# Eight batches of a conditioned transformer block on one core: maxima turned by quarters and halves, score blocks in a third bank

## What is computed

```
c6 = silu(c) @ Wc + bc                       # shifts, scales, gates
xm = ln(x) * (1 + sc_msa) + sh_msa
q, k, v = xm @ Wq + bq, xm @ Wk + bk, xm @ Wv + bv
w = softmax((q / DH) @ k.T)                  # per head, 512 x 512
x = x + g_msa * ((w @ v) @ Wo + bo)
xm2 = ln(x) * (1 + sc_mlp) + sh_mlp
x = x + g_mlp * (gelu(xm2 @ W1 + b1) @ W2 + b2)
```

## Time and profile before

| | |
|---|---|
| median of 3 runs | 773.78 us (772.47 to 776.5) |
| profiled execution | 772.2 us, its span 770.0 us |
| TensorE | 709.4 us busy (92%) |
| VectorE | 580.5 us busy (75%) |
| ScalarE | 391.1 us busy (51%) |
| GpSimd | 216.5 us busy (28%) |

### The profile page before, as it was taken

The page is one execution under the profiler, slowest core; times in us unless marked ns, Lnnn a source line. Parts: engine busy times, 40 slices in busy tenths (PEclk is TensorE's granted clock), DMA queues, the critical chain, the costliest instruction groups (busy, mean ns, idle before and its releaser), DMA issues.

```text
span 770.0 us, 11786 instructions
## 1 busy us (share of the span) xinstructions
PE 709.4 (92%) x3967; PEld 382.9 (50%) x3967; DVE 580.5 (75%) x1019; ACT 391.1 (51%) x463; POOL 216.5 (28%) x162
## 2 busy tenths in 40 slices
PE   4788989869999999999999999999999998998996
PEld 2451222432378325762478225862478225822886
DVE  4779788959896998789886798789886986721563
ACT  5420556127742775257642675257633773298221
POOL 1454020200343032512162032412162022330444
PEclk9875899869999999999999999999999999999999
DMA  8599000771058303850076303840076102021110
GB/s 295 197 262 261 22 29 20 253 170 55 29 194 207 112 15 114 252 147 29 28 239 160 102 14 131 239 143 29 29 239 166 65 27 72 3 83 44 57 35 27
DMA packets 59846, 88.45 MB, mean 115 GB/s; under 512 B 6246, under 2 KB 47740, under 8 KB 56716
## 3 DMA queue, kind: packets, MB, share of 16 engines
q1 hardware_dynamic: 59788, 87.69, 37.0%
HBM read 49.35 MB, written 38.06 MB: 114 GB/s over the span
## 4 chain that ended last, share of the span: by engine, by line
PE 35%; issue 34%; DVE 14%; POOL 11%; ACT 3%; DMA 3%; POOLq 0%; SPq 0%; ACTq 0%; DVEq 0%
DVE mx L947 7%; PE ps L651 7%; PE ps L629 7%; PE ps L574 6%; PE ps L659 5%; POOL hl L462 4%; PE ps L795 4%; PE ps L799 2%; POOL prob L452 2%; ACT prob L520 2%; DVE prob L1019 1%; POOL x L432 1%; POOL xd L445 1%; PE ps L611 1%; PE ps L731 1%
## 5 line engine op out<-in xcount | busy, mean ns | idle before, releaser
L947 DVE TENSOR_REDUCE mx<-ps 128x1 f32<-128x512 f32 x512 | 336.0, 686 | 60.8 <-PE ps L629 54.7
L520 ACT ACTIVATE prob<-ps 128x1024 f32<-128x1024 f32 x256 | 247.8, 1022 | 155.4 <-PE ps L659 155.2
L629 PE MATMUL ps<-kst,qst 96*128 96x512 bf16 x512 | 197.5, 407 | 22.5 <-DVE mx L947 17.1
L659 PE MATMUL ps<-qst,kst 98*128 98x512 bf16 x512 | 150.6, 386 | 4.2 <-DMA qst<-mrow 2.7
L629 PEld LDWEIGHTS ps<-kst,qst 96*128 96x128 bf16 x512 | 45.5, 98 | 189.8 <-DVE mx L947 165.9
L651 PE MATMUL ps<-prob,vaug 128*32 128x512 f32 x1024 | 137.8, 610 | 0.5 <-ACT prob L520 0.3
L462 POOL TENSOR_TENSOR hl<-z,hh 128x512 fp32r<-128x512 f32 x64 | 82.3, 1286 | 136.5 <-DVE hh L1079 136.5
L561 ACT ACTIVATE z<-ps,bias_t 128x512 f32<-128x512 f32 x64 | 44.0, 688 | 134.7 <-PE ps L799 129.9
L409 POOL TENSOR_TENSOR rstd<-vare,mhalf 128x4 f32<-128x4 f32 x16 | 16.7, 1046 | 255.2 <-DVE vare L875 255.2
L659 PEld LDWEIGHTS ps<-qst,kst 98*128 98x128 bf16 x512 | 47.1, 99 | 70.6 <-ACT prob L520 26.9
L452 POOL TENSOR_TENSOR prob<-prob 128x512 bf16<-128x512 f32 x32 | 38.3, 1196 | 139.8 <-DVE prob L1022 139.8
(11 more groups left out here) (106 smaller groups left out, 833.0 us busy)
## 6 DMA issues: line engine op xcount, KB each, us to landing
parts_scratch<-prob SPq DMA_DIRECT2D x32, 384.0 KB, 2.9
qst<-parts_scratch SPq DMA_DIRECT2D x16, 768.0 KB, 9.1
kst<-parts_scratch SPq DMA_DIRECT2D x16, 768.0 KB, 13.6
parts_scratch<-prob SPq DMA_DIRECT2D x32, 256.0 KB, 3.2
y_scratch<-rb SPq DMA_DIRECT2D x32, 256.0 KB, 2.0
xa<-in_x_dram SPq DMA_DIRECT2D x8, 512.0 KB, 4.3
parts_scratch<-prob SPq DMA_DIRECT2D x32, 128.0 KB, 2.9
xd<-in_x_dram SPq DMA_DIRECT2D x8, 512.0 KB, 3.5
```

Source lines behind the costliest of these rows:

```text
L520: act.activation(prob[:, s % 2, 2 * p:2 * p + 2, :], ps[:, 2 * p:2 * p + 2, :], ACT.Exp, scale=1.0 / DH).then_inc(exp_done, 1)
L629: pe.matmul(ps[:, banks[n % len(banks)], :], qst[1 - par][0:MROW, h, t * P:(t + 1) * P], kst[1 - par][0:MROW, h, :], start=True, stop=True ...
L659: m = pe.matmul(ps[:, q, :], kst[par][0:KROWS, G * g + q, kt * P:(kt + 1) * P], qst[par][0:KROWS, G * g + q, :], start=True, stop=True)
L947: dve.tensor_reduce(mx[:, t, h:h + 1], ps[:, banks[n % len(banks)], :], AXX, ALU.max).then_inc(max_done, 1)
```

## The change

The tables become one tuple of counts for each kind of step: `FIRST` for step 0, `NEXT` for step 1, `STEADY` for the others (unchanged counts). Step -1 does 18 blocks of batch 0, turns 4 heads, and does 6 more. Step 0's attention then has 40 old blocks in attention steps 0 to 9 and 24 of batch 1 in 10 to 15, with a turn of four heads in attention steps 2, 6 and 10. After the projections 2 blocks, a turn of the first eight heads of batch 1, and 12 more. Step 1's attention has the last 20 blocks of batch 1 in attention steps 0 to 5, their turn in 6, and 34 of batch 2 from 7 on, where it had 45 of batch 2; its projections have 8 blocks besides the 2 at the transposes instead of 4, its MLP 20 instead of 13. In the step of a turn, TensorE does the transposed scores, the turn, `pv`, and then the blocks.

In the attention the blocks may also go to whichever of the banks 4 and 5 collects no values (`rotation` takes the bank used longest ago), except in attention steps 0, 1, 5, 9 and 13 and for the first two blocks of 2, 6, 10 and 14, while a value bank is being emptied and the other already collects. `spare_free` makes `pv` and the projections wait for the last block in such a bank, and a wait on `y_evac` stands before the third block of an attention step 6, 10 or 14.

Beside this, x of batch 1 is loaded into tile `x1` ahead of the biases, and normalised before the third part of q and k; `write_parts` writes each of the three parts as soon as it is ready, copied to its slots from one source row; the first rows are issued between the q and the k stack of batch 1; and two waits for GpSimd fills are moved.

```diff
-C_BLOCKS = (1, 0) + (3,) * (STEPS - 4) + (4, 4)
-TURN_BLOCKS, QK_BLOCKS, V_BLOCKS = (1, 1), (0, 1, 0, 1), (0, 1, 0, 1)
-UP_BLOCKS, DOWN_BLOCKS = (1, 1, 1), (2, 2, 2, 2, 2, 0, 0, 0)
-assert sum(map(sum, (C_BLOCKS, TURN_BLOCKS, QK_BLOCKS, V_BLOCKS, UP_BLOCKS, DOWN_BLOCKS))) == NH * TT
-HALF, EXTRA = NH * TT // 2, 8
-OLD_BLOCKS = (4,) * 6 + (0,) * (STEPS - 6)
-NEW_BLOCKS = (0,) * 6 + (4,) * (STEPS - 6)
-OLD_TURN = 5
-assert HALF + EXTRA + sum(OLD_BLOCKS) == NH * TT and OLD_TURN < STEPS // 2
+QUARTER, HALF, EXTRA, SECOND = NH * TT // 4, NH * TT // 2, 8, 44
+Blocks = namedtuple("Blocks", "old new turn qk v up down")
+STEADY = Blocks((0,) * STEPS, (1, 0) + (3,) * (STEPS - 4) + (4, 4), (1, 1), (0, 1, 0, 1), (0, 1, 0, 1), (1, 1, 1), (2, 2, 2, 2, 2, 0, 0, 0))
+FIRST = Blocks((4,) * 10 + (0,) * 6, (0,) * 10 + (4,) * 6, (1, 1), (0, 1, 0, 1), (0, 1, 0, 1), (), ())
+NEXT = Blocks((2, 2, 4, 4, 4, 4) + (0,) * 10, (0,) * 7 + (3, 3) + (4,) * 7, (1, 1), (1,) * 4, (1,) * 4, (2, 2, 2), (3, 3, 3, 3, 2, 0, 0, 0))
+assert sum(map(sum, STEADY)) == NH * TT and sum(map(sum, NEXT[1:])) == NH * TT
+assert QUARTER + EXTRA + sum(FIRST.old) == NH * TT and SECOND + sum(NEXT.old) == NH * TT
...
+def rotation(stretches):
+    used = {}
+    for n, banks in enumerate(banks for banks, blocks in stretches for _ in range(blocks)):
+        bank = min(banks, key=lambda b: used.get(b, -1))
+        yield bank, n - used[bank] if bank in used else 0
+        used[bank] = n
+def attention(blocks):
+    for s, n in enumerate(blocks):
+        alone = n if s < 2 or s % TT == 1 else min(n, 2) if s % TT == 2 else 0
+        yield (6, 7), alone
+        yield (6, 7, 5 - (s - 1) // TT % 2), n - alone
+SPAN_FIRST, SPAN_NEXT, SPAN_STEADY = QUARTER + 2, SECOND - sum(FIRST.new), NH * TT
+MAX_FIRST = max_banks(((6, 7, 0, 1), SPAN_FIRST), ((6, 7), EXTRA - 2), *attention(FIRST.old))
+MAX_SECOND = max_banks(*attention(FIRST.new), ((6, 7), SPAN_NEXT), *attention(NEXT.old))
+MAX_THIRD = max_banks(*attention(NEXT.new), ((6, 7), SPAN_STEADY - sum(NEXT.new)))
+MAX_STEADY = max_banks(*attention(STEADY.new), ((6, 7), SPAN_STEADY - sum(STEADY.new)))
+FIRST_TURNS, NEXT_TURNS = {2: 4, 6: 8, 10: 12}, {6: 8}
...
+            sp.dma_start(x1[:], x[1].rearrange("(t p) f -> p t f", p=P)).then_inc(xb_loaded, 16)
...
+                def load_maxima(b, stack, head):
+                    last = heads_of(b, head)
+                    sp.wait_ge(mrow_done, 2 * turn_no(b, head))
                     for n in range(2):
-                        sp.dma_start(stack[MROW + n:MROW + n + 1, first:last, :], mrow[0:last - first, n, :]).then_inc(loaded, 16)
-                if runs(i, 0) and not later(i, 0, 1):
-                    sp.wait_ge(mrow_done, 2)
-                    load_maxima(qst[par], NH // 2, NH, m_loaded)
+                        sp.dma_start(stack[MROW + n:MROW + n + 1, head:last, :], mrow[0:last - head, n, :]).then_inc(m_loaded, 16)
                 if runs(i, 0):
+                    if at(i, 0):
+                        load_maxima(i, qst[par], 4)
...
                     for g in range(NG):
                         sp.wait_ge(y_evac, NG * i + g + 1)
                         sp.dma_start(y_scr[G * g:G * (g + 1)].rearrange("h r s -> (h r) s"), ysb[:, g % 2, :]).then_inc(y_written[g % 2], 16)
+                        if g == 0 and (at(i, 0) or at(i, 1)):
+                            load_maxima(i, qst[par], 8)
+                        if g == 1 and at(i, 0):
+                            load_maxima(i, qst[par], 12)
...
                 def write_parts(b, j):
-                    sp.wait_ge(part_l, 4 * b + j + 1)
-                    for slot, part, n in SLOT_RUNS[j // 2]:
-                        sp.dma_start(parts_scr[j, slot:slot + n].rearrange("n p s -> p n s"), parts[:, j, part:part + n, :])\
-                            .then_inc(parts_written[j], 16)
+                    for part, ready in enumerate((part_h, part_m, part_l)):
+                        at, step, n = PART_SLOTS[j // 2][part]
+                        sp.wait_ge(ready, 4 * b + j + 1)
+                        sp.dma_start(parts_scr[j, at:at + (n - 1) * step + 1:step].rearrange("n p s -> p n s"),
+                                     parts[:, j, part, :].unsqueeze(1).broadcast_to([P, n, S])).then_inc(parts_written[j], 16)
...
+                        load_maxima(0, qst[1 - par], 0)
                         sp.wait_ge(const_set, 5)
                     load_stack(i + 2, 1, 0)
                     load_stack(i + 2, 1, 1)
-                if early(i) and runs(i, 1):
-                    sp.wait_ge(half_rows, 2)
-                    load_maxima(qst[1 - par], 0, NH // 2, half_loaded)
-                elif runs(i, 1):
-                    sp.wait_ge(mrow_done, 2 * i + 4)
-                    load_maxima(qst[1 - par], 0, NH, m_loaded)
+                if runs(i, 1) and not early(i):
+                    load_maxima(i + 1, qst[1 - par], 0)
...
+            spare_used = {}
+            def spare_free(bank):
+                if bank in spare_used:
+                    pe.wait_ge(max_done, spare_used.pop(bank))
+            def scores(i, par, blocks):
+                banks, back = max_of(i + 1)
                 for _ in range(blocks if runs(i, 1) else 0):
                     n = block_at[0]
                     block_at[0] = (n + 1) % (NH * TT)
                     h, t = n // TT, n % TT
-                    if n >= len(banks):
-                        pe.wait_ge(max_done, 64 * (i + 1) + n - len(banks) + 1)
+                    if back[n]:
+                        pe.wait_ge(max_done, 64 * (i + 1) + n - back[n] + 1)
                     if t == 0 and h % 8 == 0:
                         pe.wait_ge(stack_loaded[h // 8], 32 * (i + 2))
-                    if n == 0:
-                        if later(i, 1, 1):
-                            pe.wait_ge(mrow_done, 2 * (i + 1))
-                    pe.matmul(ps[:, banks[n % len(banks)], :], qst[1 - par][0:MROW, h, t * P:(t + 1) * P], kst[1 - par][0:MROW, h, :],
+                    if t == 0 and h in (8, 12) and at(i + 1, 0):
+                        pe.wait_ge(mrow_done, 2 * turn_no(0, h - 4))
+                    elif t == 0 and h == 8 and at(i + 1, 1):
+                        pe.wait_ge(mrow_done, 2 * turn_no(1, 0))
+                    elif n == 0 and later(i, 1, 1):
+                        pe.wait_ge(mrow_done, 2 * (turn_no(i + 1, 0) - 1))
+                    if banks[n] in (4, 5):
+                        spare_used[banks[n]] = 64 * (i + 1) + n + 1
+                    pe.matmul(ps[:, banks[n], :], qst[1 - par][0:MROW, h, t * P:(t + 1) * P], kst[1 - par][0:MROW, h, :],
                               start=True, stop=True).then_inc(s_done, 1)
...
+            def turn_maxima(b, head, bank=6):
+                if runs(b, 0):
+                    last = heads_of(b, head)
+                    pe.wait_ge(max_done, 64 * b + TT * last)
                     if bank == 4:
                         pe.wait_ge(vaug_done, 4)
                     for t in range(TT):
-                        m = pe.transpose(ps[0:last - first, bank, t * P:(t + 1) * P], mx[:, t, first:last], ident[:])
-                    m.then_inc(turned, 1)
+                        m = pe.transpose(ps[0:last - head, bank, t * P:(t + 1) * P], mx[:, t, head:last], ident[:])
+                    m.then_inc(mt_done, 1)
...
+                    spare_free(4 + g % 2)
...
-                        pe.wait_ge(const_set, 6)
+                        pe.wait_ge(const_set, 3)
...
-                        if s == STEPS // 2 and not later(i, 0, 1):
-                            pe.wait_ge(m_loaded, 32)
+                        if s in (4, 8, 12) and at(i, 0) or s == 8 and at(i, 1):
+                            pe.wait_ge(m_loaded, 32 * turn_no(i, s))
                         for p in range(2):
                             if s:
                                 pe.wait_ge(exp_done, 32 * i + 2 * s - 1 + p)
                                 transposed_scores(i, par, s, p)
-                            if later(i, 0, 1):
+                            if turn is None and not at(i, 0):
                                 between(p, p + 1)
-                            elif p == 1:
+                            elif turn is None and p == 1:
                                 between(0, 2)
+                        if turn is not None:
+                            turn_maxima(i, turn)
                         if s:
                             pv(i, par, s - 1)
+                        if turn is not None:
+                            between(0, 2)
+                        if s > TT and s % TT == 2 and has_b:
+                            pe.wait_ge(y_evac, NG * i + s // TT)
                         between(2, old + new)
-                        if s == OLD_TURN and not later(i, 0, 1):
-                            turn_maxima(i - 1, NH // 2, NH)
...
-                    scores(i, par, HALF + 2, (6, 7, 0, 1))
```

(51 more changed lines are left out.)

112 lines of the change are left out of this document (58 added, 54 removed).

## The result

The changed kernel takes **783.24 us** (median of 4 runs, 781.63 to 784.65) against 774.41 for the one before: a ratio of 1.0101, 95% interval 1.0071 to 1.0132. I had forecast 776 and a range of 766 to 782. Two more comparisons of the unchanged pair, made beside experiments, gave 1.0113 (1.0075 to 1.0150) and 1.0099 (1.0069 to 1.0130).

The account below looks back on a forecast made before the run. TensorE bounds steady attention; VectorE or DMA bounds other stretches. Start -10.2, step 0's attention +1.5, its tail -0.6, step 1 +13.3, steady steps -1.5 sum to +2.5 on 773.8: 776 us, range 766 to 782.

Parts of the forecast that it names:

- Step 1 takes the 20 blocks: Step 1: the moved blocks lengthen it by +13.3 us, bounds +5.5 to above +16; sum of (a) to (f) less 1.5.
- (a): Step 1, attention steps 0 and 1: third block waits for VectorE's maxima behind the residual, delaying step 2's scores, +2.5 us.
- (b): Step 1, attention steps 2 to 5: VectorE's 16 maxima and seven normalisation pieces exceed the former time, +2.7 us or less.
- (c): Step 1, attention step 6: the turn, without blocks of its own, costs 1.0 us of wait and transposes.
- (d): Step 1, attention steps 7 to 15: 34 blocks instead of 29, alternating between TensorE's and VectorE's pace, +1.6 us.
- (e): Step 1, Q/K/V and up: seven more maxima on a VectorE 94% busy, +3.8 us.
- (f): Step 1, down products: four get a third block in two banks, 4 x 0.8 = +3.2 us.
- second rival: Step 0, attention steps 2 to 5: TensorE's clock stays low after a turn's wait, +6.8 us, 783; chance 0.11.
- The start: Before the first attention: earlier normalisation and 16 fewer blocks, partly lost waiting for rows behind Q loads, -10.2 us (-12.8 to -8.0).
- The tail: Tail of step 0: DMA-bound, so fewer blocks gain nothing; only the earlier first part does, -0.6 us (0 to -1.5).
- The steady steps: Steady steps: the third bank removes 0.3 us of bank wait in five batch-pipeline steps, -1.5 us (0 to -4).
- The first rival: Step 1: the moved blocks hide under TensorE, so it costs +5.5 us and the kernel takes 768.5; chance 0.25.

Follow-up runs that it names:

- the experiment: Changed kernel with step 1's down products at 2,2,2,2,2 score blocks instead of 3,3,3,3,2, the four moved to attention steps 7 to 15: 778.34 us, 1.0049.
- Undoing the halves: Changed kernel with batch 1's maxima turned once, all 64 of its blocks in step 0, and step 1 at the steady step's counts: 772.00 us, 0.9952.
- the best kernel: Kernel with one turn for batch 1, its 34 score blocks in step 0's tail rotating over four banks instead of two: 768.99 us, 0.9922.

## Why the prediction was wrong

**The step that failed is "Step 1 takes the 20 blocks"**, +13.3 where the trace has +19.45; its upper bound was open ("above +16"). Its parts, by the prediction's letters:

- (a), attention steps 0 and 1: +2.5 forecast, +5.49 read. The place and the wait were right. I priced the wait and the work behind it at full clock; the work behind it ran at half. Where the clock was at full behind the same wait, the two steps still cost +3.4 and +3.9, so the term was too small by some 1 us even then. What decides whether the clock is low behind a wait is not shown.
- (b), attention steps 2 to 5: +2.7 or less forecast, +1.37 read (172.65 to 184.50, 11.85 against 10.48). The third bank helps here: with two banks this stretch of step 1 took 13.08. It took 12.58 in the second profile of the changed kernel, where the clock was at half nearly as long, so between 0.5 and 1.2 of the difference is the bank's.
- (c), the turn: 1.0 forecast, 0.21 read (2.83 for that step).
- (d), attention steps 7 to 15: +1.6 forecast, +2.64 read.
- (e), Q/K/V and up: +3.8 forecast, +5.65 read. I counted maxima on a full VectorE. The larger part was waits of 0.66 and 2.72 us and the value products at half clock after them. With four blocks fewer both were gone, but the up products returned 2.3; VectorE's load was real as well. The cast behind the longer wait stood in the kernel before at the same length, and I had not looked for a slow operation ahead of the moved maxima.
- (f), down: 4 x 0.8 forecast, 4 x 0.97 measured by the experiment. Mis-sized by a fifth, of which 0.07 was my rounding: 0.65 of wait plus 0.22 are 0.87.

The mechanism of my second rival, TensorE's clock, was thus part of the miss of 6.15, but in step 1, where I had not looked for it. How much is an estimate: the low clock behind the first wait is worth 0.9 to 2.7 us by the profiles with and without it; in the projections of the second profile the clock was at half for 3.4 us in place of 6.8, and they took 21.33 in place of 22.18, so the 6.8 us are worth some 1.7. That this rival's 783 us is the measured time is chance: its own condition did not come. In step 0, where I had put it, the clock was back at 1.00 from 77 on and attention cost +1.74, against +1.5 forecast. There the parts fit too: with two banks this attention took 1.62 more, where I had 1.8 for the third bank, which leaves 3.4 for the turns against 3.3. The exponentials around the first turn, which lies between the second line and the third:

```profile
71.64 1.94 ACT L571 ACTIVATE prob<-ps 128x1024 f32<-128x1024 f32 x2 [2.11 <-PE ps L725]
76.88 1.94 ACT L571 ACTIVATE prob<-ps 128x1024 f32<-128x1024 f32 x2 [3.30 <-PE ps L725]
81.31 1.94 ACT L571 ACTIVATE prob<-ps 128x1024 f32<-128x1024 f32 x2 [2.49 <-PE ps L725]
84.15 1.94 ACT L571 ACTIVATE prob<-ps 128x1024 f32<-128x1024 f32 x2 [0.89 <-PE ps L725]
```

**The start** was right in kind. The first score block came 1.94 us earlier (47.72 against 49.66) where I had 3.2; over all profiles with this start it came 1.5 to 4.1 earlier. TensorE waited 2.91 us for the rows, which landed behind the Q loads as I had said:

```profile
66.47 1.87 PE L725 MATMUL ps<-qst,kst 98*128 98x512 bf16 x4 [2.91 <-DMA qst<-mrow]
```

The start gave 8.55 in place of 10.2, and 8.3 to 9.9 over the fourteen other profiles with this start (66.26 to 67.82). The normalisation took 1.37 us for its four pieces in the new place (26.65), not the 3.23 of the row; GpSimd did nothing from 25.64 to 29.22. That is what I had expected by the rule that VectorE's two-port modes and GpSimd take turns at a shared port pair (the Trainium skill, SBUF — State Buffer, Who interferes with whom). The same rule bears on (e), and the trace agrees: the cast of 2.54 us began 0.09 us behind a GpSimd subtraction of 2.35 and ended 0.28 behind it. The bound of -8.0 for the slow normalisation should read -8.3 by its own terms.

**The tail** has the wrong sign, -0.6 against +1.08; the seven profiles with this tail and the load right behind are all longer than the kernel before's one, by 0.1 to 3.7. Up to the K loads' issue it is 0.2 shorter, from there on 1.3 longer. I had seen that it was bound by transfers and had not asked what else would now be in the queue: the x load of batch 3, which went out at 160.82 before the change, 10.1 us behind the K loads, follows them by 2.6 now. That this load is the cause is not shown; the experiments leave its cost between nothing (the times) and 2.6 us (the tails of 41.62 and 39.01). My 1 us for 384 KB was low besides: at the 262 GB/s of the earlier trace rows it is 1.5.

**The steady steps** gave 0.9 of the 1.5 (0.75 and 1.9 in the two other profiles of the changed kernel).

**The first rival** (the blocks hide under TensorE) is refuted: they cost step 1 almost 1 us each. What was in it is the 0.2 us that a fourth block costs in an attention step, seen when the down blocks, or those of the projections, went there. My signs could not catch this miss: I had set a floor for step 1's growth (9 us) and no ceiling. The attention "near 48 us" was counted from 167.85 to 209.68; counted so it grew to 51.7 (161.69 to 213.35), and the 48.23 of the table is no hit.

**What the parts are worth.** Undoing the halves gains 11.5 us (1.0101 to 0.9952 of 775), undoing the third bank loses 5. The start's 8.55 us are real, but with one turn for batch 1 the tail returns 8.3 of them (48.83 against 40.54), since 16 blocks of batch 0 that were ahead of the first attention now stand in it, and as many of batch 1 move from it into the tail. In the best kernel that is where four banks win back part.
